# Sixteen samples of a two-layer transformer block on one core: a written order of stages for each engine in place of a computed one, weight slots by load order, no idle multiplications

## What is computed

```python
def layer0(x, mod, context):                       # x, context: (16, 256, 256)
    sh_a, sc_a, g_a, sh_c, sc_c, g_c, sh_m, sc_m, g_m = split(silu(mod) @ w_ada + b_ada)
    h = ln(x) * (1 + sc_a) + sh_a
    q, k, v = roll(h @ w_qkv + b_qkv, -64).windows(128)        # "w"
    x = x + g_a * (roll(softmax(q @ k.T / 4) @ v, 64) @ w_so + b_so)
    h = ln(x) * (1 + sc_c) + sh_c
    s = (h @ w_q + b_q) @ k(context).T / 4                     # "t"
    top, at = top_k(s, 16)
    x = x + g_c * (softmax(top) @ v(context)[at] @ w_co + b_co)
    h = ln(x) * (1 + sc_m) + sh_m
    x = x + g_m * ((silu(h @ w_a) * (h @ w_b)) @ w_m2 + b_m2)  # "m", hidden 1024
    return x

def layer1(x, context, cond):
    q = ada_ln(x, cond) @ Wq + bq                              # "n4"
    k, v = split(ada_ln(context, cond) @ Wkv + bkv)            # "nc"
    return x + softmax(q @ k.T / 4) @ v @ Wp + bp              # "l"
```

## Time and profile before

| | us |
|---|---|
| median of 3 runs | 1319.04 |
| lowest, highest | 1315.83, 1323.58 |
| span of the profiled execution | 1318.7 |
| TensorE busy in it | 1221.3 (93%) |
| VectorE busy | 1162.2 (88%) |
| ScalarE busy | 994.5 (75%) |
| GpSimd busy | 849.7 (64%) |

### The profile page before, as it was taken

One profiled execution on the slowest core, in us unless ns is written; L12 is line 12 of the kernel. 1 busy time (PEld: TensorE's weight loads), 2 busy tenths in 40 slices (PEclk: granted clock), 3 DMA queues, 4 the chain that ended last, 5 costly groups with the idle time before them and its releaser, 6 DMA issues. The chain is left out here.

```text
span 1318.7 us, 38821 instructions
## 1 busy us (share of the span) xinstructions
PE 1221.3 (93%) x13667; PEld 860.3 (65%) x13667; DVE 1162.2 (88%) x3854; ACT 994.5 (75%) x2001; POOL 849.7 (64%) x1134
## 2 busy tenths in 40 slices
PE   6888798999999999999999999999999999989897
PEld 5665476667676766666676766676676766656564
DVE  4469899999999999998999999999999999897443
ACT  3644487879797978878797979888797878776754
POOL 1314397958686886859496877959595868666310
PEclk8768799999999999999999999999999999989999
DMA  6531111202111121202121121312030211110110
GB/s 202 139 94 32 36 39 40 66 22 69 39 50 50 29 79 34 65 19 71 30 58 43 42 66 26 82 28 66 17 85 23 74 26 34 34 26 17 34 34 17
DMA packets 111390, 67.23 MB, mean 51 GB/s; under 512 B 13837, under 2 KB 107871, under 8 KB 111199
## 3 DMA queue, kind: packets, MB, share of 16 engines
q1 hardware_dynamic: 109166, 63.71, 18.2%
q10 hardware_dynamic: 2032, 1.05, 0.3%
HBM read 22.33 MB, written 4.19 MB: 20 GB/s over the span
## 5 line engine op out<-in xcount | busy, mean ns | idle before, releaser
L1762 ACT ACTIVATE prob<-turned_score 128x1024 f32<-128x1024 f32 x320 | 325.9, 1018 | 115.5 <-PE turned_score L1434 107.4
L2021 POOL TENSOR_TENSOR pair<-full,pair 128x512 f16<-128x512 f32 x182 | 210.6, 1163 | 108.5 <-ACT pair L1727 100.3
L2027 POOL TENSOR_SCALAR far<-far 128x512 bf16<-128x512 bf16 x256 | 158.0, 617 | 110.9 <-DVE far L1937 92.3
L1923 DVE MATCH_REPLACE8 rest<-top,score 128x256 f32<-128x256 f32 x512 | 207.7, 413 | 0.0
L1937 DVE MATCH_REPLACE8 far<-best,rest 128x256 bf16<-128x256 f32 x512 | 205.3, 408 | 1.0 <-issue 1.0
L1920 DVE MAX8 top<-score 128x8 f32<-128x256 f32 x512 | 192.2, 416 | 6.8 <-PE score L1434 6.4
L1910 DVE TENSOR_REDUCE rowmax_l<-score 128x4 f32<-128x1024 f32 x121 | 147.3, 1217 | 42.0 <-PE score L1434 29.4
L1434 PE MATMUL work<-pair_n,w_m_hi 128*128 128x256 f16 x1024 | 173.5, 274 | 1.4 <-ACT pair_n L1727 1.3
L1434 PE MATMUL work<-pair_n,w_m_lo 128*128 128x256 f16 x512 | 139.8, 273 | 0.0
L1727 ACT ACTIVATE pair<-full 128x512 f16<-128x512 f32 x192 | 121.0, 630 | 18.7 <-DMA q_stack_l<-pair 1.0
L1434 PEld LDWEIGHTS work<-pair_n,w_m_hi 128*128 128x128 f16 x1024 | 96.1, 98 | 22.3 <-issue 9.9
(11 more groups left out here) (206 smaller groups left out, 3190.9 us busy)
## 6 DMA issues: line engine op xcount, KB each, us to landing
k_stack_t<-pair SPq DMA_DIRECT2D x96, 64.0 KB, 2.3
k_stack_l<-pair SPq DMA_DIRECT2D x96, 64.0 KB, 2.3
k_stack_w<-pair SPq DMA_DIRECT2D x93, 64.0 KB, 2.3
q_stack_w<-pair SPq DMA_DIRECT2D x93, 64.0 KB, 2.3
q_stack_t<-pair SPq DMA_DIRECT2D x93, 64.0 KB, 2.3
q_stack_l<-pair SPq DMA_DIRECT2D x93, 64.0 KB, 2.3
ctx_t<-in_ctx_turned SPq DMA_DIRECT2D x16, 256.0 KB, 2.8
ctx_l<-in_ctx SPq DMA_DIRECT2D x16, 256.0 KB, 2.9
```

Of the source, the lines that this page charges most:

```text
L1762: act.activation(prob[:, at:at + 2, :], both_b[:, :, :], ACT.Exp).then_inc(exp_done, 1)
L1923: m = dve.match_replace(rest[p % 2][:, t, :], eight[:, t, :], bank[:, t * L:(t + 1) * L], -FAR)
L2021: pool.tensor_tensor(pr[:, 1, :, :], whole[:, :, :], pr[:, 0, :, :], ALU.subtract).then_inc(split_lo, 1)
L2027: pool.tensor_scalar(tile, tile, FAR, -1.0, ALU.add, ALU.mult).then_inc(far_fixed, 1)
```

## The change

Three things. First, `orders` reads a dictionary `ORDERS` with the stages of each engine written out, in place of the tables, start ticks and shifts. Each engine has exactly the same stages as before, but in another order: not in fill and drain alone, nearly half of TensorE's stages stand 1 to 12 places from where they stood. Second, the slot of a weight chunk goes by the order in which SyncE loads the chunks, and the waits for it are counted accordingly. Third, `IDLE_WORK` is empty. What the stages issue is otherwise the same.

```diff
-IDLE_WORK = ("a_w:0:3=12 o_w:0:1=19 bk_w:0:0=18 x4_n2:0:0=26 wp:0:17=13 a_w:1:0=7 a_t:0:0=22 a_w:1:3=14 "
...
-             "pr_l:15:0=35")
+IDLE_WORK = ("")
...
-def orders(B, chunks):
-
-    window_at, top_at, middle_at, last_at = starts(B)
-    rows, moved = [], shifts()
...
-                rows.append((row[0] + at[b] + moved.get((row[2], b, row[3]), 0.0), k, b, row))
-    rows.sort(key=lambda e: (e[0], e[2], e[1]))
-    return {e: [(row[2], b, row[3]) for _, _, b, row in rows if engine_of(row, b) == e]
-            for e in ("sp", "pe", "act", "dve", "pool")}
+ORDERS = {
...
+        "bk_w:0 pj_tk:0 pj_wq:1 pr_w:0 wp:0:14 xt_w:0 vj_w:1 pj_wk:1 x4_n2:0 pj_tq:0 wp:0:17 a_w:1 wp:0:19 a_w:1:1 "
...
+def orders():
+
+    found = {}
+    for engine, text in ORDERS.items():
+        found[engine] = []
+        for one in text.split():
+            stage, b, item = (one + ":0").split(":")[:3]
+            found[engine].append((stage, int(b), int(item)))
+    return found
...
-        slot_of = [k if k < NSTAGE else (k - NSTAGE) % NLATE for k in range(len(chunks))]
...
-        plan = orders(B, chunks)
+        plan = orders()
+        loads = [k[2] for k in plan["sp"] if k[0] == "wd"]
+        load_no = {k: j for j, k in enumerate(loads)}
+        slots = [j if j < NSTAGE else (j - NSTAGE) % NLATE for j in range(len(loads))]
+        slot_of = {k: slots[j] for k, j in load_no.items()}
+
+        def loads_in_slot(k):
+            return slots[:load_no[k] + 1].count(slot_of[k])
...
-                    if i >= NSTAGE:
-                        before = max(k for k in range(i) if slot_of[k] == slot_of[i])
-                        sp.wait_ge(lo_done, wl_no["wl", 0, before])
+                    if load_no[i] >= NSTAGE:
+                        before = max(j for j in range(load_no[i]) if slots[j] == slot_of[i])
+                        sp.wait_ge(lo_done, wl_no["wl", 0, loads[before]])
...
-                    pe.wait_ge(stage_in[slot_of[i]], 16 * (slot_of[:i].count(slot_of[i]) + 1))
+                    pe.wait_ge(stage_in[slot_of[i]], 16 * loads_in_slot(i))
...
-                        dve.wait_ge(hi_done, 1 + sum(c[0] == "wt" for c in chunks[:i]))
+                        dve.wait_ge(hi_done, wh_no["wh", 0, i])
```

More of the change, by code:

```diff
@@ L154, in stage_rows @@
-def stage_rows(table):
-    rows = []
-    for engine, text in table:
-        for one in text.split():
-            name, _, tick = one.partition("@")
-            stage, _, item = name.partition(":")
-            rows.append((float(tick), engine, stage, int(item)))
-    return rows
-def window_rows():
-    return stage_rows(WINDOW)
-def top_rows():
-    return stage_rows(TOP)
-def middle_rows():
-    return stage_rows(MIDDLE)
-def last_rows():
-    return stage_rows(LAST)
-def weight_rows(chunks):
-    return stage_rows(WEIGHTS)
@@ L184, in starts @@
-def starts(B):
-    window = (-72.12069, -8.15504, 55.95335, 119.96857, 184.03617, 247.96045, 312.06351, 375.9032, 439.99275,
-              504.06725, 567.81508, 632.0068, 695.87912, 759.8787, 823.80732, 887.9397)
-    top = (-0.0124, 63.99337, 127.99713, 191.9508, 256.04932, 319.98339, 383.98487, 447.90361, 511.83636,
-           575.89402, 639.86889, 703.87411, 767.88139, 831.8858, 895.89022, 959.89321)
-    middle = (75.92701, 140.00486, 204.00672, 267.91975, 331.85495, 395.71788, 459.95595, 524.07272,
-              587.99893, 651.83061, 715.96035, 779.86918, 843.88793, 907.91364, 971.82381, 1035.85571)
-    last = (151.99307, 215.88107, 279.99322, 343.98852, 407.86164, 471.95094, 535.91077, 599.88377,
-            663.91731, 727.87353, 791.87264, 855.9005, 919.90344, 983.88216, 1047.88371, 1112.4173)
-    return window, top, middle, last
@@ L198 @@
-SHIFTS = {
[772 rows of a table removed]
-}
-def shifts():
-    found = {}
-    for b, text in SHIFTS.items():
-        for one in text.split():
-            name, _, tick = one.partition("@")
-            stage, _, item = name.partition(":")
-            found[stage, b, int(item)] = float(tick)
-    return found
-IDLE_WORK = ("a_w:0:3=12 o_w:0:1=19 bk_w:0:0=18 x4_n2:0:0=26 wp:0:17=13 a_w:1:0=7 a_t:0:0=22 a_w:1:3=14 "
-             "o_w:1:0=8 a_t:0:3=8 bk_w:1:0=9 pr_w:1:0=7 xt_w:1:0=13 a_t:0:6=21 pr_t:0:0=15 o_w:2:3=10 "
-             "a_t:1:3=17 x4_n4:14:0=13 xt_t:15:0=14 a_l:14:3=10 ot_l:13:0=6 xt_m:15:0=17 x4_n4:15:0=18 "
-             "o_l:14:2=34 a_l:15:0=10 bk_l:14:0=8 a_l:15:3=11 a_l:15:4=11 a_l:15:5=14 o_l:15:3=17 bk_l:15:0=18 "
-             "pr_l:15:0=35")
+ORDERS = {
[130 rows of a table added]
+    "act": (
[96 rows of a table added]
+    "dve": (
[74 rows of a table added]
+    "pool": (
[84 rows of a table added]
+}
@@ L998, in idle_work @@
     return found
-def orders(B, chunks):
-    window_at, top_at, middle_at, last_at = starts(B)
-    rows, moved = [], shifts()
-    for k, row in enumerate(weight_rows(chunks)):
-        rows.append((row[0] + WEIGHTS_AT, k, 0, row))
-    for at, group in ((window_at, window_rows()), (top_at, top_rows()), (middle_at, middle_rows()),
-                      (last_at, last_rows())):
-        for b in range(B):
-            for k, row in enumerate(group):
-                rows.append((row[0] + at[b] + moved.get((row[2], b, row[3]), 0.0), k, b, row))
-    rows.sort(key=lambda e: (e[0], e[2], e[1]))
-    return {e: [(row[2], b, row[3]) for _, _, b, row in rows if engine_of(row, b) == e]
-            for e in ("sp", "pe", "act", "dve", "pool")}
+def orders():
[6 more added lines that the diff above has]
+    return found
 def weight_chunks(C, HID):
@@ L1169, in build @@
         wl_no = number("dve", "wl")
+        wh_no = number("act", "wh")
         assert [(k[0][2:], *k[1:]) for k in b_no] == [(k[0][2:], *k[1:]) for k in e_no]
@@ L1370, in _ @@
                 if kind == "wd":
-                    if i == NSTAGE:
+                    if load_no[i] == NSTAGE:
                         for row in (0, 32):
@@ L1756, in _ @@
                     if n <= NPROB // 2:
-                        act.wait_ge(lo_done, max(wl_no["wl", 0, k] for k in range(NLATE, NSTAGE)))
+                        act.wait_ge(lo_done, max(wl_no["wl", 0, k] for k in loads[NLATE:NSTAGE]))
                     if n > NPROB // 2:
```

89 lines of the change are left out of this document (1 added, 88 removed), and 1156 rows, old and new, of tables (ORDERS, SHIFTS).

## The result

The changed kernel took 1302.28 us (median of 4 runs, 1301.36 to 1313.5) against 1317.43 for the kernel before, run beside it (4 runs, 1314.32 to 1323.58). The ratio, which is one of means, is 0.9899, with a 95% interval of 0.9855 to 0.9943: 1.0% faster, 13 us. A second comparison with more executions gave 0.9917 (0.9886 to 0.9947), 11 us, with a median of 1308.12 against 1320.08. Single executions of one kernel differ by up to 15 us, so a time of one execution says little here, and the next sections count by stretches of several profiles.

What follows compares the result with a forecast made beforehand. The long middle was taken as bound by two full engines, TensorE and VectorE, fill and drain by chains of waits. -9.3 + 2.0 - 2.9 + 1.7 - 0.5 = -9.0 from 1318.7, and 0.3 to the median: 1310 us, range 1298 to 1323.

Steps and rivals of the forecast that it cites:

- (a): VectorE's order in the middle: 29 instead of 39 places where it waits ahead of a row maximum, -9.3 us.
- (b): SyncE's queue: top-k query stacks behind guard rows at four samples, four x loads or stores ahead of guards, +2.0 us.
- (c): Fill: earlier first top-k row, a weight subtraction moved away, no wait ahead of the first divisions, -2.9 us.
- (d): Idle multiplications gone: last attended product starts 0.7 us sooner, tail at 1.2 GHz costs 2.4, net +1.7 us.
- (e): Rest of the drain: last sample's second MLP projection a few rows earlier, the rest nearly as it was, -0.5 us.
- Rival C: More than summed: price of the 29 places left falls from 0.64 to 0.4, fill gives -5; 1301 us, chance 0.15.
- the price of a place: In the middle, VectorE's wait where two readers of the score pair stand next to each other: 0.64 us each.
- Rival A: Stalls change places: VectorE waits somewhere else, the middle gives only 0 to -3 us; 1317 us, chance 0.27.
- The working's 0.2: Sample 5's top-k query stack, issued behind the guard row, reaches its reader at 419.1, 0.2 us behind 418.92.
- the odd one: VectorE's 3.65 us wait at 617.54, where three x loads delayed a guard row; counted in the -9.3 us.
- Rival B: Slower by the clock: without idle multiplications TensorE falls to 1.2 GHz in fill and drain; 1331 us, chance 0.13.
- (f): Weight slots by load order: waits for the previous load's split, over by 85 us and counted within the fill.

Runs made afterwards that it cites:

- dve_swap: Kernel before, with VectorE's addition to x moved between the second and third row maximum at seven window samples (5 to 11); ratio 0.9965, -4.6 us.
- fill_only: Kernel before, with the new order for stages begun in the first 200 us and the fill's idle multiplications gone; ratio 0.9976.
- first_back: Changed kernel, with the old order and idle multiplications for stages begun in the first 83 us; ratio 0.991.
- nv_back: Changed kernel, with VectorE's first division back ahead of second halves 4 and 5 of sample 0's top-k; ratio 0.9897.
- no_idle: Kernel before with its order, and none of the 475 idle multiplications; ratio 1.0023, +3 us.

## Why the prediction was right, and where its steps were off

The forecast was 1310 us and faster by 9.0; the median is 1302 by the first comparison and 1308 by the second, and the ratios say 11 to 13 us faster. Its direction and range hold. By the table, measured less forecast is +1.3 us for (a) and (b) together, -2.3 for (c), +2.8 for (d) and -6.8 for (e). The two largest errors have opposite signs, so that the sum came within 5 us of the table's -14.0 is in part luck. Rival C, more than the sum, named 1301 us, nearer to the first comparison's median; its reasons are not what the rows show, since the price of a place in the middle did not fall to 0.4 us (20.2 / 29 = 0.7), and most of what came beyond the forecast came in the drain.

(a) *VectorE's order in the middle* fits as the mechanism, and by its own rows is nearly the right number: 18.6 us of idle time ahead of row maxima forecast, 20.2 read. Two things in it were wrong. The 3.65 us of the earlier trace rows were taken as the kernel's, and were more than half one execution's; against the executions without it (22.1 and 22.7 us from sample 2 to 14) the row maxima gave 3 to 4 us. And a covered place was taken to cost nothing, where it keeps 0.3 of 0.55 us (dve_swap). The stretch still gained 6.0, since other rows gained too: VectorE's whole idle time there went from between 28 and 31 us down to between 22 and 26. Rival A (stalls only change places) does not describe the whole change: no other wait of VectorE in the middle grew by more than 1 us. For single places it is not excluded, since dve_swap's trace is no shorter than fill_only's. By the orders 923 of TensorE's 1639 stages moved, which is more than half and not nearly half.

(b) *SyncE's queue* was forecast at +2.0 and has the other sign. The stacks behind the guard did arrive late, three times, 1.2 us in all, near the 0.2 to 0.5 each of the working (in other profiles of the new order up to 1.5 at one place). The working's 0.2 came from adding's 2.50 us to the end of the stack's issue, though they run from the start of an issue; from the start of its last transfer it would have been nothing. But TensorE waited for guard rows for 1.7 to 3.5 us an execution in before's order, and waits for at most 1.0 now. The step counted the x loads and stores that moved ahead of guard rows, and not what moved behind them, save the odd one. Apart from the load of x at 615 us (0.6 to 2.4 us of TensorE's wait) there is a second place, which neither the prediction nor its rows have: the third guard row of sample 11 stood behind the six transfers of a key stack and a context load. TensorE waited for it 0.8 to 2.2 us in the five profiles with that order, and VectorE 1.0 to 2.4 us for the score behind it in three of them. SyncE's queue and TensorE in dve_swap, which has it at its worst:

```profile
906.42 3.97 SPq L893 DMA_DIRECT2D k_stack_w<-pair  x6
910.44 1.73 SPq L883 DMA_DIRECT2D ctx_l<-in_ctx  x1
912.27 0.55 SPq L899 DMA_DIRECT2D q_stack_t<-guard_t  x1
...
914.55 0.39 PE L923 MATMUL turned_score<-q_stack_t,k_stack_t 49*128 49x256 f16 x4 [2.22 <-DMA q_stack_t<-guard_t]
```

In the changed kernel the guard row is issued ahead of the key stack, and the multiplication behind it (906.44) waits for no transfer:

```profile
901.29 0.55 SPq L871 DMA_DIRECT2D q_stack_t<-guard_t  x1
901.88 2.08 SPq L847 DMA_DIRECT2D x_tile<-in_x  x3
904.13 3.82 SPq L865 DMA_DIRECT2D k_stack_w<-pair  x6
```

(c) *Fill.* The sum of durations gave 82.2 us for the first top-k row, and it came at 82.39; over all profiles that stretch scatters by nearly 6 us (79.3 to 85.0), so an agreement to 0.2 is chance, and no edit in it can be told (first_back). The subtraction that moved away was priced at 0.5; in the changed kernel GpSimd's two tiny instructions take 1.07 and 0.19 us in place of 1.07 and 1.05, so it was worth 0.9 on GpSimd. Behind it, the moved division gave 3.2 us (nv_back) in place of 1.5: the term was the wait of one execution, 1.54, while the other profiles with that order have 1.6 to 2.3 and nv_back 2.9.

(d) *Idle multiplications.* The tail was forecast at +1.7, with a warm start of the last attended product and a cold tail. The profile of the changed kernel has +1.4 for the projection and nothing for the transposes, which ran at 2.4 GHz and not at the forecast 1.2; over six profiles the last stretch is 4.5 us longer. The step that failed is that only the last 12 us were looked at, and not the whole 50, in which the clock also falls (a mean of 0.87 to 0.66); nor were the four groups ahead of that stretch counted, whose absence may have given 3 us back. Rival B named this mechanism, and in the drain some of it happened, at a fifth of its price at most; in the fill it is not seen.

(e) *Rest of the drain*, -0.5, is the step that was most wrong: -7.3 us, of which some 3 may belong to idle multiplications. It read the order there as nearly unchanged and followed one chain. By the means about 2.5 us are ahead of sample 15's last top-k row (VectorE idle for 4.3 to 5.9 us from sample 14's first on, instead of 7.2 to 9.7), and 4.7 behind it, in the last MLP. There TensorE of before stood still in the middle of the chain, for a stack of another sample (timeline of before; the same wait is 1.43 us in no_idle):

```profile
1236.95 0.39 PE L1434 MATMUL turned_score<-q_stack_l,k_stack_l 49*128 49x256 f16 x4
1239.30 0.39 PE L1434 MATMUL score<-k_stack_l,q_stack_l 48*128 48x256 f16 x4 [1.96 <-DMA q_stack_l<-pair]
1239.63 0.39 PE L1434 MATMUL work<-pair_n,w_m_hi 128*128 128x256 f16 x2
```

In the changed kernel the MLP's third part runs first and the score behind it:

```profile
1221.30 0.38 PE L895 MATMUL work<-pair_n,w_m_hi 128*128 128x256 f16 x2
...
1221.62 0.38 PE L895 MATMUL work<-pair_n,w_m_hi 128*128 128x256 f16 x2
...
1223.07 0.39 PE L895 MATMUL score<-k_stack_l,q_stack_l 48*128 48x256 f16 x4
```

From the same stage on either side the changed kernel gains 2.8 us here (1239.63 - 1221.62 against 15.2 ahead of it). The next 1.2 come behind it, where scores of other samples moved behind the second projection and two idle groups are gone; no run parts these two. That row is TensorE's longest wait in the last 100 us of before, so a list of them by length would have shown it ahead of time.

(f) Weight slots: nothing to see on either side, as said.

## What to carry to other kernels

A wait is worth its price only as a mean over executions: take the same place in several periods or profiles before a single long one is put into a sum. When two whole orders are compared by hybrids, the seam has a price of its own (here 4 us, a late context load), and only stretches away from it can be read. In a drain, follow every wait of the engine that carries the last chain, also those for other samples' data, and look at the granted clock over the whole drain, and not only in its last few us.

## What the runs showed of the hardware

SyncE's issue of the same three loads of x at the same place took 2.25 to 2.99 us in five executions, and 1.5 to 3.1 at other places. One context load took 0.59 us in one execution and 1.73 in another, at the same place (916 us in before, 910 in dve_swap). The granted clock of the same sequence of multiplications without idle work came out at 0.87, 0.79 and 0.66 in three executions. The stretch in which the second was read took 50.6, 53.4 and 56.7 us, in the last case with one stage of VectorE's moved far ahead of it and nothing else changed.
